# A mixture-of-experts stage on one core: token rows transposed by a DMA instead of by TensorE

## The reference, cut to what is computed

```
x = x + tanh(g_xattn) * gelu(LN(x) @ ctx.T) @ ctx          # per batch of 224 tokens
xf = LN(x); scores = softmax(xf @ gate_w); top 2 of 8 kept  # scale[t, e]
h  = silu((scale * xf) @ w1[e]) * ((scale * xf) @ w3[e])    # 512 -> 256
x  = x + tanh(g_ffn) * sum over e of h @ w2[e]              # 256 -> 512
```

## Time and profile before

| | us |
|---|---|
| median of 3 runs | 695.38 (694.34 to 696.14) |
| profiled execution, span from first to last instruction | 703.6 |
| mean granted TensorE clock | 0.987 |
| PE busy | 641.4 (91%) |
| ACT busy | 461.6 (66%) |
| DVE busy | 417.0 (59%) |
| POOL busy | 403.9 (57%) |
| DMA: indirect queue / SP's queue, share of 16 engines | 27.0% / 32.5% |

### The profile page before, as it was taken

One profiled execution on the slowest core, in us unless ns is written; L12 is line 12 of the kernel. 1 busy time (PEld: TensorE's weight loads), 2 busy tenths in 40 slices (PEclk: granted clock), 3 DMA queues, 4 the chain that ended last, 5 costly groups with the idle time before them and its releaser, 6 DMA issues.

```text
span 703.6 us, 15832 instructions
## 1 busy us (share of the span) xinstructions
PE 641.4 (91%) x4638; PEld 443.4 (63%) x4639; DVE 417.0 (59%) x1287; ACT 461.6 (66%) x771; POOL 403.9 (57%) x459
## 2 busy tenths in 40 slices
PE   2799999899999999999898999989999999999990
PEld 1677788777877877778785555444554555545550
DVE  3457878888778887797796644453333333333330
ACT  5999999998988989889874344334443444344440
POOL 4422545765666656665566586765555555555551
PEclk9999999999999999999999999999999999999996
DMA  7546557756586567655433566656665766666653
GB/s 213 148 142 188 153 155 155 197 139 183 137 188 160 163 141 195 168 150 166 121 102 88 102 121 115 97 91 119 117 109 106 118 113 109 115 116 115 112 105 55
DMA packets 51380, 94.77 MB, mean 135 GB/s; under 512 B 17024, under 2 KB 25344, under 8 KB 51312
## 3 DMA queue, kind: packets, MB, share of 16 engines
q1 hardware_dynamic: 34096, 60.02, 32.5%
q0 software_dynamic: 16400, 33.89, 27.0%
q10 hardware_dynamic: 816, 0.02, 0.1%
HBM read 61.89 MB, written 32.01 MB: 133 GB/s over the span
## 4 chain that ended last, share of the span: by engine, by line
DMA 24%; PE 12%; issue 6%; DVE 4%; POOL 2%; POOLq 1%; ACT 1%; DVEq 1%; SPq 0%; ACTq 0%
DMA out_rows<-ctx_raw,meta 21%; PE bank L1369 6%; PE bank L1378 3%; DMA ctx_raw<-xf_rows,meta 2%; POOL out_rows L537 2%; PE bank L1324 1%; POOLq L533 1%; PE bank L1358 1%; ACT ctx_raw L766 0%; DMA meta<-route_table 0%; PE bank L1258 0%; POOL ctx_raw L525 0%; PE bank L1223 0%; DVE ctx_part L825 0%; DVEq L1155 0%
## 5 line engine op out<-in xcount | busy, mean ns | idle before, releaser
L1369 PE MATMUL bank<-w,ctxT 128*128 x756 | 175.2, 382 | 0.9 <-issue 0.9
L537 POOL DMA_INDIRECT out_rows<-ctx_raw,meta x63 | 100.3, 1592 | 103.4 <-DMA out_rows<-ctx_raw,meta 91.2
L1223 PE MATMUL bank<-ctx_part,a_part 125*112 125x512 f16 x576 | 135.1, 380 | 0.1
L1211 PE MATMUL bank<-xnT,ctxT 128*125 128x224 f16 x1152 | 120.7, 262 | 2.4 <-DVE xnT L855 1.9
L1369 PEld LDWEIGHTS bank<-w,ctxT 128*128 128x128 f16 x756 | 74.3, 98 | 77.1 <-issue 3.4
L1211 PEld LDWEIGHTS bank<-xnT,ctxT 128*125 128x125 f16 x1152 | 112.2, 138 | 2.8 <-DVE xnT L855 2.2
L777 ACT ACTIVATE ctxT<-bank,cols 128x256 f32<-128x256 f32 x63 | 29.8, 473 | 121.6 <-issue 103.9
L1223 PEld LDWEIGHTS bank<-ctx_part,a_part 125*112 125x112 f16 x576 | 71.4, 130 | 39.1 <-DVE a_part L834 0.3
L629 ACT ACTIVATE ctxT<-bank 128x1000 f16<-128x1000 f16 x96 | 94.4, 1005 | 1.4 <-PE bank L1178 1.4
L1378 PE MATMUL bank<-w2s,ctxT 128*128 x378 | 91.9, 379 | 1.3 <-DVE ctxT L1138 1.3
L489 POOL DMA_INDIRECT route_table<-route,pos_i x64 | 72.7, 1136 | 19.2 <-issue 17.8
(11 more groups left out here) (155 smaller groups left out, 1026.4 us busy)
## 6 DMA issues: line engine op xcount, KB each, us to landing
ctx_raw<-in_ctx SPq DMA_DIRECT2D x48, 448.0 KB
w_raw<-in_L_ffn_w SPq DMA_DIRECT2D x24, 512.0 KB
x<-in_x SPq DMA_DIRECT2D x16, 448.0 KB, 6.5
out_rows<-x SPq DMA_DIRECT2D x16, 448.0 KB
xf_rows<-xf SPq DMA_DIRECT2D x16, 448.0 KB
ctx_raw<-in_ctx SPq DMA_DIRECT2D x48, 52.0 KB
meta<-route_table SPq DMA_DIRECT2D x66, 1.0 KB
ctx_raw<-xf_rows,meta POOLq DMA_INDIRECT x66
```

Of the source, the lines that this page charges most:

```text
L537: g.indirect_dma_start(out=out, out_offset=bass.IndirectOffsetOnAxis(ap=meta[n][:, 0:1], axis=0), in_=y_sb[n % 2], in_offset=None, compute ...
L1211: ins = t_.matmul(dst, ctxT[u][:, hc * KD + k, c * CS:c * CS + CR], xnT[u][:, hx, k, :], start=j == 0, stop=j == KD * len(PARTS) - 1)
L1223: ins = t_.matmul(O_ps[t][0:TT, :], a_part[ha][:, c, t * TT:(t + 1) * TT], ctx_part[u][hc][:, c, :], start=c == 0 and (ha, hc) == PARTS[0] ...
L1369: ins = t_.matmul(H_ps[u][:, :], rows, w, start=m == 0, stop=m == KD * len(PARTS) - 1)
```

## The change

The gathered fp32 rows are split into their two fp16 halves as rows, before any transpose: ACT casts (`rows_high`) and DVE takes the remainder (`rows_low`), both now from the gathered rows in SBUF into `xh`, two blocks ahead (`SPLIT`) instead of one. SP then issues one transposing DMA per block (`turn_rows`), 128 x 1024 fp16 (256 KB) from SBUF to SBUF, into one of three buffers. PE's `trans_rows` is gone, and `up` waits for the DMA. There are four buffers of gathered rows, and POOL gathers four blocks ahead, once the split of block b is done. SP issues all first 12 index loads, one `store_norm`, and then the first two transposing DMAs; from then on each step has one transposing DMA two blocks ahead and one index load eight blocks ahead (`META`), all written out. `sg` and `hh` move to another buffer.

```diff
@@ -53 +53 @@
 TRASH = E * EB
 NB = (T * TOPK) // P + E - 1
 PEEL = 3
-AHEAD = 3
+AHEAD = 4
 PEEL2 = 27
+SPLIT = 2
+META = 8
 APART = 3
 MAPPED = 12 * S * TOPK
 NBM = NB + AHEAD
@@ -133 +135 @@
         g_raw = sb("g_raw", [P, 2])
         g_tanh = sb("g_tanh", [P, 2])
         ctx_raw = sb("ctx_raw", [P, NC, D])
-        ctx_part = [[sb(f"ctx_part{u}{h}", [CR, NC, D], F16) for h in range(2)] for u in range(2)]
+        ctx_part_buf = [[sb(f"ctx_part{u}{h}", [P, NC, D], F16) for h in range(2)] for u in range(2)]
+        ctx_part = [[b[0:CR, :, :] for b in of_batch] for of_batch in ctx_part_buf]
         ctxT_buf = [sb(f"ctxT{u}", [P, 2 * KD * NC * CS], F16) for u in range(2)]
         ctxT = [b[:, :].rearrange("p (g c) -> p g c", g=2 * KD) for b in ctxT_buf]
         ctx_sum = sb("ctx_sum", [P, NQ])
@@ -185 +188 @@
         taken = xn[0:1, 1, 128:128 + E]
         m_e, m_r, m_t, m_same = (xn[0:1, 0, n * NBM:(n + 1) * NBM] for n in range(4))
         bmap = sb("bmap", [1, 3, NBM], I32)
-        bidx, landed_at, mapped, m_base = (xn[0:1, 0, lo:lo + n] for lo, n in ((4 * NBM, NBM), (5 * NBM, NBM + 2), (6 * NBM + 2, E + 1), (6 * NBM + E + 3, 1)))
+        bidx, landed_at, mapped, m_base = (xn[0:1, 0, lo:lo + n] for lo, n in ((4 * NBM, NBM), (5 * NBM, NBM // 2 * 2 + 2), (6 * NBM + 2, E + 1), (6 * NBM + E + 3, 1)))
         cnt_mapped = sb("cnt_mapped", [1, E])
         meta_all = sb("meta", [P, RING, 2], I32)
         meta = [meta_all[:, n, :] for n in range(RING)]
@@ -198 +201 @@
 
         xg = [ctx_raw[:, a, :] for a in range(AHEAD)]
         y_sb = [ctx_raw[:, AHEAD + u, :] for u in range(2)]
-        xgT = [[ctxT_buf[u][:, h * KD * P:(h + 1) * KD * P] for h in range(2)] for u in range(2)]
-        sg, hh = (words[u][:, 1024:1024 + HID].bitcast(F32) for u in range(2))
+        xh = [ctx_part_buf[0][0][:, 2 * u:2 * u + 2, :] for u in range(2)]
+        xgT_buf = [ctxT_buf[0][:, r * 2 * KD * P:(r + 1) * 2 * KD * P] for r in range(3)]
+        xgT = [[b[:, h * KD * P:(h + 1) * KD * P] for h in range(2)] for b in xgT_buf]
+        sg, hh = (words[1][:, 1024 + n * HID:1024 + (n + 1) * HID].bitcast(F32) for n in range(2))
         hhT = [ctxT_buf[0][:, 4096 + h * KH * P:4096 + (h + 1) * KH * P] for h in range(2)]
 
         bank = [ps(f"bank{n}", [P, 512]) for n in range(8)]
@@ -245 +250 @@
         tables_loaded = sem("tables_loaded")
         meta_loaded = [sem(f"meta_loaded{n}") for n in range(RING)]
         gathered = [sem(f"gathered{a}") for a in range(AHEAD)]
-        xgT_made, xgT_ready = sem("xgT_made"), sem("xgT_ready")
-        xgT_high, hhT_high = sem("xgT_high"), sem("hhT_high")
+        rows_cast, rows_split, hhT_high = sem("rows_cast"), sem("rows_split"), sem("hhT_high")
+        xgT_loaded = [sem(f"xgT_loaded{r}") for r in range(3)]
         up_made, sg_ready, hh_ready = sem("up_made"), sem("sg_ready"), sem("hh_ready")
         hhT_made, hhT_ready = sem("hhT_made"), sem("hhT_ready")
         y_made, y_ready = sem("y_made"), sem("y_ready")
@@ -370 +375 @@
 
             def load_meta(b, n, half):
 
-                if not (isinstance(b, int) and b < RING):
+                if b >= RING:
                     sp.wait_ge(added[n % 2], half * 16 - (RING // 2 - 1) * 16)
                 row = sp.value_load(bmap[0:1, 1, bass.ds(b, 1)], min_val=0, max_val=TRASH)
                 sp.dma_start(meta[n][:, :], table[bass.ds(row * P, P), :]).then_inc(meta_loaded[n], 16)
 
-            for b in range(AHEAD):
+            def turn_rows(b, n):
+
+                sp.wait_ge(rows_split, b + 1)
+                if b >= 3:
+                    sp.wait_ge(up_made, b - 2)
+                sp.dma_start_transpose(xgT_buf[n % 3].rearrange("p (g r) -> p g r", g=2 * KD),
+                                       xh[n % 2].rearrange("p h d -> p (h d)")).then_inc(xgT_loaded[n % 3], 16)
+
+            for b in range(RING):
                 load_meta(b, b, b // 2)
             store_norm(B - 2)
-            for b in range(AHEAD, RING):
-                load_meta(b, b, b // 2)
-            store_rows(B - 1)
-            store_norm(B - 1)
-            for b in range(RING, PEEL2):
-                load_meta(b, b % RING, b // 2)
-            sp.wait_ge(x2_stored, 16 * B)
-            sp.wait_ge(xf_stored, 16 * B)
-            sp.wait_ge(map_ready, 2)
-            for v in range(2):
-                sp.wait_ge(routed[v], 16 * 2 * TOPK * B // 2)
-            sp.nop().then_inc(phase2, 1)
-            for b in range(PEEL2, PEEL2 - PEEL2 % RING + RING):
-                load_meta(b, b % RING, b // 2)
-            with sp.Fori(PEEL2 // RING + 1, NBM // RING) as it:
-                for n in range(RING):
-                    load_meta(it * RING + n, n, it * (RING // 2) + n // 2)
-            for b in range(NBM - NBM % RING, NBM):
-                load_meta(b, b % RING, b // 2)
+            for b in range(SPLIT):
+                turn_rows(b, b)
+            for b in range(PEEL2):
+                turn_rows(b + SPLIT, b + SPLIT)
+                if b == 0:
+                    store_rows(B - 1)
+                elif b == 4:
+                    store_norm(B - 1)
+                if b + META == PEEL2:
+                    sp.wait_ge(x2_stored, 16 * B)
+                    sp.wait_ge(xf_stored, 16 * B)
+                    sp.wait_ge(map_ready, 2)
+                    for v in range(2):
+                        sp.wait_ge(routed[v], 16 * 2 * TOPK * B // 2)
+                    sp.nop().then_inc(phase2, 1)
+                if b + META >= RING:
+                    load_meta(b + META, (b + META) % RING, (b + META) // 2)
+            for b in range(PEEL2, NB):
+                if b + SPLIT < NB:
+                    turn_rows(b + SPLIT, (b + SPLIT) % RING)
+                if b + META < NBM:
+                    load_meta(b + META, (b + META) % RING, (b + META) // 2)
...
@@ -561 +577 @@
                     inv_std(mv2, 2, mv2_ready, rstd2_ready, B)
 
             def step2(b, n, lap, half):
-                pool.wait_ge(xgT_made, b + 1)
+                pool.wait_ge(rows_split, b + 1)
                 if isinstance(b, int) and b + AHEAD == PEEL2:
                     pool.wait_ge(phase2, 2)
                 gather(b + AHEAD, (n + AHEAD) % RING, lap + (n + AHEAD) // RING)
@@ -729 +745 @@
 
             batches(act, step)
 
-            def rows_high(b, u):
-
-                act.wait_ge(xgT_made, b + 1)
-                a.activation(xgT[u][0], T_ps[u][:, :], ACT.Copy, scale=2.0 ** X_BITS).then_inc(xgT_high, 1)
+            def rows_high(b, n, lap):
+
+                act.wait_ge(gathered[n % AHEAD], lap * (16 * RING // AHEAD) + 16 * (n // AHEAD + 1))
+                if n >= SPLIT:
+                    act.wait_ge(xgT_loaded[(n - SPLIT) % 3], lap * (16 * RING // 3) + 16 * ((n - SPLIT) // 3 + 1))
+                a.activation(xh[n % 2][:, 0, :], xg[n % AHEAD], ACT.Copy, scale=2.0 ** X_BITS).then_inc(rows_cast, 1)
 
             def last_step(i, u, h):
 
@@ -749 +767 @@
                 act.wait_ge(a_ready, B * NQ)
                 a.activation(g_raw[:, 0:1], g_raw[:, 1:2], ACT.Silu).then_inc(tables_loaded, 1)
                 xfT_out(i * 4 + 1, 1)
-                rows_high(0, 0)
+                for b in range(SPLIT):
+                    rows_high(b, b, 0)
 
             last_step(B - 1, 1, (B - 1) // 2)
 
@@ -769 +788 @@
                 first_, u = isinstance(b, int) and b == 0, n % 2
                 if not first_:
                     hid_high(b - 1)
-                rows_high(b + 1, 1 - u)
+                rows_high(b + SPLIT, n + SPLIT, lap)
                 act.wait_ge(cols_ready, b + 1)
                 act.wait_ge(up_made, b + 1)
                 if not first_:
@@ -1069 +1088 @@
                 one(v.tensor_tensor(m_same[:, 0:rest], m_same[:, 0:rest], m_t[:, 0:rest], ALU.mult))
                 land_map(PEEL2, rest)
 
-            def rows_low(b, u):
-
-                dve.wait_ge(xgT_high, b + 1)
-                v.scalar_tensor_tensor(xgT[u][1], T_ps[u][:, :], 2.0 ** X_BITS, xgT[u][0], ALU.mult, ALU.subtract).then_inc(xgT_ready, 1)
+            def rows_low(b, n):
+
+                dve.wait_ge(rows_cast, b + 1)
+                v.scalar_tensor_tensor(xh[n % 2][:, 1, :], xg[n % AHEAD], 2.0 ** X_BITS, xh[n % 2][:, 0, :], ALU.mult, ALU.subtract).then_inc(rows_split, 1)
 
             def last_step(i, u, h):
 
@@ -1089 +1108 @@
                 split_begin(weight_low, i, u, h)
                 a_low(i, u, 2)
                 route_scores(i - 3, 1 - u)
-                rows_low(0, 0)
+                for b in range(SPLIT):
+                    rows_low(b, b)
                 route_top(i - 2)
 
             last_step(B - 1, 1, (B - 1) // 2)
@@ -1148 +1168 @@
                 v.tensor_copy(cols[u][:, 2:3], Q[:, bass.ds(e * 3 + 2, 1)]).then_inc(cols_ready, 1)
                 if not first_:
                     hid_low(b - 1)
-                rows_low(b + 1, 1 - u)
+                rows_low(b + SPLIT, n + SPLIT)
                 dve.wait_ge(cols_ready, b + 1)
```

(25 more changed lines are left out.)

## The result

The changed kernel takes 716.5 us (median of 4, 710.1 to 719.3) against 695.05 before: ratio 1.030, 95% interval 1.025 to 1.035. The forecast was 687, with a range of 678 to 735. It is slower by 21 us where 8 less were forecast. A second set of four gave 712.9 (ratio 1.029, 1.022 to 1.037). The profiled execution shown here took 710.1, with a span of 708.4; it is the quickest of its four.

What follows compares the result with a forecast made beforehand. The prediction took PE as the bound, with POOL's chain showing at changes of expert. It summed +8 (start) - 3 (391 to 477) - 11 (477 to 655) - 2 (655 to 693) = -8, so 687 us, range 678 to 735.

Steps and rivals of the forecast that it cites:

- The bound before: From 477 to 655 us: PE bounds, with POOL's chain showing at each change of expert; 38 x 4.54 plus 6.7 us waits.
- PE's step without row transposes: PE's step per block in phase 2: 0.22 + 2.59 + 1.35 = 4.16 us, 0.38 saved from 4.54.
- The gain from 477 to 655, 17 us before contention: Late stretch, 38 steps: 14.4 us from PE's shorter step plus 3 from fewer waits for gathered rows.
- The transposing DMA: SP's 256 KB transposing DMA per block: 1.0 us of all engines, ends 0.7 and 4.6.
- rival B: Phase 2: transposing DMA takes 2 to 3 us, DMA bounds, steps 5 to 6 us, PE waits for xgT; about 735; chance 0.22.
- Against the rest of the traffic: From 477 to 655 us: DMA share 0.96 delays landings, charged 0.15 us a block, 6 us, ends 0 and 15.
- The start: Block 0 of phase 2 starts 6.4 us later behind twelve index loads, plus 1.7 for the lower clock: +8 us.
- near 389: Sign that the forecast is right: `up` of block 0 begins near 389 us, at half clock; before, 382.57.
- The rest: Other stretches: 391 to 477 us saves about 3, 655 to 693 saves 2, SP's moved stores and index loads 0.
- Mechanism A: Rival: DMA contention delays scatters by 1 us and more, costing 15 us instead of 6; 696 to 700; chance 0.18.
- D: Rival: transposing DMA lands after more than 7 us, ACT waits for `xh`, step of 5; about 710; chance 0.07.
- C: Rival: late start absorbed as POOL catches up from 391 to 477 us, +8 becomes +3; 679 us; chance 0.13.

Runs made afterwards that it cites:

- e_four: The kernel before with four buffers of gathered rows instead of three, gathers four blocks ahead, TensorE transposes kept: 688.8 us, ratio 0.992.
- e_noturn: The changed kernel with only blocks 0 to 2 turned by the DMA, later blocks multiplying stale rows: 687.8 us, ratio to before 0.990.

## Why the prediction was wrong

**The bound before** was read rightly: PE, with late rows at changes of expert. Removing only those (`e_four`) gave 5 us (688.8 against 694.1 for the kernel before beside it), 3 of them in the 37 steps; 6.7 were counted there.

**PE's step without row transposes.** Forecast 0.22 + 2.59 + 1.35 = 4.16; undisturbed steps take 4.22. Right as the length of a step that waits for nothing.

**The gain from 477 to 655, 17 us before contention: failed.** Without turned rows 37 steps took 167.5 us against 173.3, a gain of 6. I had covered lateness of gathers, which held (3.2 us), and let POOL catch up, but never followed the late scatter back to `y_out`, which waits for the scatter two before it. In the four-buffer kernel at 4.60 a step ACT waits for it 2.6 us in 2 places; without row transposes 17.5 us in 12. With four result buffers the gain is 12 of the 17. The last 5, net, are not explained.

**The transposing DMA: the step that failed first.** I took 1.0 us of all 16 engines, "since the source rows are long and a plain transfer is the nearest in size". It measures 1.64, in pieces of 256 bytes, past the 1.2 that rival B named as the point from which DMA decides. The row of 32-byte pieces pointed to the right kind of mechanism, a price per piece (26 ns here, and half the pieces took 0.74 us). The rule of the Trainium skill that the prediction quoted (Advanced Engine Details and Errata, X-Bar Transpose: about 90% of a plain copy) does not hold here: 0.74 us plain, 1.64 turned, 45%.

**Against the rest of the traffic: failed with it.** I charged 6 us, with 15 as the end, because PE was to stay the bound and pay only at changes of expert. Measured are 25 to 29, by `e_noturn` against the two sets, and PE is no longer the bound. Scatters land a median of 5.8 us after issue for 4.8 to 4.9, and a change of expert costs 6.9 for 5.6.

**The start** was right in kind and a little too dear: +8 forecast, +6.6 measured from first load to scatter 0. Block 0's up comes 4.4 us later after the first load (17.9 for 13.5), not 6.4, as the twelve index loads took 13.0 us and not 14.2; the lower clock costs 2.2, not 1.7. The mark "near 389" failed (379.72), because the profile it was counted from had the longer phase 1. **The rest**: 391 to 477 was to save 3 and saved 1.4 without turning; with it that stretch loses 4 to 8. 655 to 693 was to save 2 and saved 3 without turning.

Summed with the measured terms, in profiles from first load to last scatter: +6.9 (start) - 1.4 - 5.8 - 3.1 = -3.4 without turning, as `e_noturn` shows, and +19.7 to +22.4 for turning: +16 to +19. The medians say +21 and +19.

**The rivals.** Mechanism A (late scatters and gathers) came, but dearer than its 15 us. B came in part: 1.64 us lies past its deciding 1.2 and under its 2 to 3, and the share is over 0.9. PE waiting for the turned rows, B's and D's mark, did not come: 6.1 us in 4 places. C's time did not come; whether the start can be absorbed is not shown. That 716.5 lies within the range is luck: the range was drawn out for B, whose price and mark are others.

## What to carry to other kernels

Work moved from an engine at 98% to a resource at 64% must be priced on that resource for the whole step: here 2.9 + 1.6 = 4.5 us of DMA against a step that was to take 4.2. Before a step is shortened, every buffer whose release hangs on a DMA landing has to be followed with the new step length. And a change of several parts is worth running part by part: its least noted one, the fourth gathered buffer, is worth 5 us by itself, nearly all that the whole change could give without its DMAs.

## What the runs showed of the hardware

A transposing DMA from SBUF to SBUF, 128 x 1024 fp16, ran as over 1000 packets and took 1.64 us of all 16 engines beside the gathers and scatters, 2.2 times a plain copy of the same bytes (0.74), and nearly in proportion to its size (0.74 for half). SP spent 1.26 us issuing one, 1.22 for half and 0.47 for the plain copy. At equal busy time the transposing DMA of half the bytes cost the kernel more than the plain copy did (15 against 8 us); why is open.
